# Linear attention on one core: an inverse ahead of the gelu phase, a value projection ahead of the MLP's later products

## What is computed

```python
for i in range(8):                                   # layers
    residual = x
    Q  = elu(x @ Wq[i] + bq[i]) + 1                  # 128 -> 1024
    Kf = elu(x @ Wk[i] + bk[i]) + 1
    V  = x @ Wv[i] + bv[i]
    KV, sumK = sum_tokens(Kf * V), sum_tokens(Kf)
    Z  = 1.0 / (Q * sumK + 1e-06)                    # the "inverse"
    att = Q * KV * Z
    y = gelu(att @ Wo[i] + bo[i])
    x = layer_norm(y + residual)
    h = gelu(x @ W1[i] + b1[i])                      # 128 -> 512
    x = layer_norm(gelu(h @ W2[i] + b2[i]) + x)
```

## Time and profile before

| | us |
|---|---|
| median of three runs | 4429.74 |
| profiled execution | 4422.76 |
| its span | 4421.0 |
| stage of linear attention (624 to 3066) | 2442 |

### The profile page before, as it was taken

How to read it: one execution, slowest core, us unless ns; L and a number is a source line. 1 busy time by engine, 2 the same in 40 slices (tenths; PEclk the granted TensorE clock), 3 DMA queues, 4 the chain that set the end, 5 groups by cost and what they waited for, 6 DMA issues and landing times.

```text
span 4421.0 us, 65537 instructions
## 1 busy us (share of the span) xinstructions
PE 3926.3 (89%) x15924; PEld 2196.2 (50%) x15924; DVE 3355.7 (76%) x10808; ACT 3129.1 (71%) x5783; POOL 1507.2 (34%) x2843
## 2 busy tenths in 40 slices
PE   5688879999999999999999999998698659999976
PEld 3466744444444444444444444443365447777745
DVE  5898579888878888788788887886666756665668
ACT  3455348999989899999899898998142426666654
POOL 2222124444444344444444344443210113333320
PEclk8888789999999999999999999999799779999988
DMA  2212110010000000000000000000000001111100
GB/s 54 34 30 40 19 24 1 1 22 3 10 16 1 17 9 1 21 6 1 23 3 8 18 1 16 11 1 1 0 1 1 0 14 44 45 44 41 43 6 19
DMA packets 152078, 71.90 MB, mean 16 GB/s; under 512 B 109576, under 2 KB 142684, under 8 KB 151666
## 3 DMA queue, kind: packets, MB, share of 16 engines
q1 hardware_dynamic: 144738, 63.96, 5.9%
q10 hardware_dynamic: 6928, 3.41, 0.3%
HBM read 54.55 MB, written 12.80 MB: 15 GB/s over the span
## 4 chain that ended last, share of the span: by engine, by line
PE 62%; DVE 15%; ACT 12%; issue 7%; POOL 1%; DMA 1%; ACTq 0%; DVEq 0%; SPq 0%; POOLq 0%
PE bank L2013 20%; PE bank L2028 7%; PE bank L2797 5%; PE bank L2057 5%; PE bank L2067 3%; PE bank L2830 2%; DVE arena L1460 2%; PE bank L613 2%; DVE arena L1464 2%; ACT L2151 2%; ACT arena L2105 2%; ACT arena L2108 2%; ACT arena L2117 2%; ACT arena L2104 2%; PE bank L2857 1%
## 5 line engine op out<-in xcount | busy, mean ns | idle before, releaser
L2013 PE MATMUL bank<-arena 128*128 128x512 f32 x3072 | 1422.5, 596 | 13.5 <-DVE arena L2194 12.0
L2013 PEld LDWEIGHTS bank<-arena 128*128 128x128 f32 x3072 | 585.9, 191 | 756.3 <-issue 722.3
L2254 POOL TENSOR_SCALAR arena<-arena 128x256 f32<-128x256 f32 x1024 | 480.4, 479 | 1190.9 <-DVE arena L2187 1190.9
L2028 PE MATMUL bank<-arena 128*128 128x512 f32 x1024 | 525.0, 604 | 62.7 <-DVE arena L2217 62.4
L2176 DVE SCALAR_TENSOR_TENSOR arena<-arena 128x256 f32<-128x256 f32 x1024 | 394.2, 422 | 195.8 <-ACT arena L2105 188.6
L2217 DVE SCALAR_TENSOR_TENSOR arena<-arena 128x256 f32<-128x256 f32 x1024 | 492.2, 525 | 13.7 <-issue 12.7
L2194 DVE SCALAR_TENSOR_TENSOR arena<-bank,bv,arena 128x256 f32<-128x256 f32 x1024 | 445.4, 473 | 0.0
L2104 ACT ACTIVATE arena<-bank,bqk 128x512 f32<-128x512 f32 x512 | 347.9, 680 | 76.9 <-PE bank L2013 68.4
L2187 DVE SCALAR_TENSOR_TENSOR arena<-bank,bq,arena 128x512 f32<-128x512 f32 x512 | 384.3, 751 | 18.1
L2117 ACT ACTIVATE arena<-arena,const_table 128x512 f32<-128x512 f32 x512 | 374.6, 732 | 0.0
L2108 ACT ACTIVATE arena<-bank,bqk 128x512 f32<-128x512 f32 x512 | 353.7, 691 | 0.9 <-PE bank L2013 0.8
(11 more groups left out here) (389 smaller groups left out, 7193.9 us busy)
## 6 DMA issues: line engine op xcount, KB each, us to landing
arena<-packed_dram SPq DMA_DIRECT2D x96, 96.0 KB
arena<-packed_dram SPq DMA_DIRECT2D x32, 288.0 KB
arena<-diag_dram SPq DMA_DIRECT2D x16, 256.0 KB, 3.8
arena<-in_L_attn_Wk_dram SPq DMA_DIRECT2D x16, 256.0 KB, 3.5
arena<-in_L_attn_Wq_dram SPq DMA_DIRECT2D x16, 256.0 KB, 4.2
arena<-in_L_attn_Wv_dram SPq DMA_DIRECT2D x16, 256.0 KB, 4.9
arena<-in_L_attn_Wo_dram SPq DMA_DIRECT2D x8, 512.0 KB, 3.9
arena<-in_L_attn_W_dram SPq DMA_DIRECT2D x16, 256.0 KB, 2.9
```

Of the source, the lines that this page charges most:

```text
L2013: nc.tensor.matmul(bank[:, RING1[m % 5], :], w1p[k][:, i * P:(i + 1) * P], zT_of(g), start=True, stop=True).then_inc(a1_proj.sem, 1)
L2028: nc.tensor.matmul(bank[:, 6, :], wo1[:, i, :], a1_att[:, i % 4, :], start=(i == 0), stop=(i == NB1 - 1)).then_inc(a1_outd.sem, 1)
L2254: last = nc.gpsimd.tensor_scalar(a, a, 1.0, a1_ksum[:, i % 4, b:b + 1], ALU.add, ALU.mult)
```

## The change

Two steps change their place in the lists of a turn; no operation is added or removed. On ScalarE `inv_act(2)` stands ahead of the gelu phase of the turn (behind exp 4) and no more behind exp 5. On TensorE the value product of block 5 stands directly behind its key and query products, ahead of hidden products 1 to 3, and no more behind them.

```diff
                 for w in range(NB1):
-                    pe.append((0, proj_pe(w, "kq" if w == 5 else "kqv")))
+                    pe.append((0, proj_pe(w)))
...
                     if w == 5:
-                        pe += [(2, h_pe((1, 2, 3))), (0, proj_pe(5, "v")), (3, turn_in_pe(1))]
+                        pe += [(2, h_pe((1, 2, 3))), (3, turn_in_pe(1))]
                         of(pe, out_pe, 0)
...
                     act.append((0, exp_act(w)))
                     if w == 4:
+                        of(act, inv_act, 2)
                         act += [(1, gelu_table_act), (3, h2_act), (1, y_act), (2, h_act), (1, exp_table_act)]
-                    if w == 5:
-                        of(act, inv_act, 2)
                     if w == 6:
                         of(act, inv_act, 3)
                         act.append((3, norm_act(1)))
```

## The result

| | before | after |
|---|---|---|
| median | 4427.72 us | 4468.36 us |
| span of the profiled execution | 4421.0 us | 4465.3 us |
| first to last gelu table load (63 turns) | 2391.34 us | 2430.09 us |

The change makes the kernel slower: ratio 1.009, 95% interval 1.0072 to 1.0107. The medians lie 40.6 us apart. Of the 44.3 us between the two spans 3.25 us lie ahead of the stage, where both kernels run the same code (ScalarE's first table load of the stage is at 623.79 us before and at 627.04 us after), and about 1 us lies behind the stage's last gelu table load.

A forecast was written before the change was run, and what follows sets the result against it. ScalarE's loop of 37.41 us bounds the turn, TensorE's 37.18 close behind; the change makes TensorE's 38.47. Terms 29.7 + 11.7 + 1.4 + 5 + 1 = 48.8 us on the 4429.74 median give 4479 us, range 4458 to 4508.

The forecast's parts named there:

- 28 turns without bias copies: Four turns per layer in layers 2 to 8: from 37.41 to 38.47 us, +1.06 each, 29.7 in all.
- 21 turns with them: Three turns per layer with ScalarE's bias copies: 113.74 to 115.41 us, +1.67 per layer, 11.7 in all.
- 7 layer ends: Turns over the layer loop's end: +0.2 us each, 1.4 in all, each bounded by 0 and 1.29.
- 6 turns of layer 1: Layer 1's turns of 37.02 us, partly shorter: +0.56 to +1.06 each where full, 5 us taken for the six.
- filling of the pipeline: The first new inverse adds about 1 us at the start of the pipeline.
- The ring: Loop exp 4, inverse, gelu phase, exp 5, VectorE, out product 2, projections, exp 4: 17.87 + 16.33 + 1.14 + 3.13 = 38.47 us.
- What out product 2 waits for: On TensorE: it waits for exp 5 through feature 5 and att 2, not for block 2's inverse, ended 0.87 us earlier.
- The value product: Block 5's, on TensorE ahead of hidden products 1 to 3: fills a wait, costs nothing, at most its 0.86 us.
- The clock: TensorE's granted clock: no falls expected behind about 1.5 us idle; the skill's rule would give 4585 us.
- Rival (a): TensorE's clock falls at the longer wait: one turn in three, 4514 us, chance 0.09; every turn, 4585 us, chance 0.01.
- signs: In the new profile: exp 0 waits 0.7 to 0.8 us, exp 4 about 0.2, hidden products 0.2 to 0.6.
- rival (b): No difference: ScalarE's loop of 37.41 us stays the bound, 4430 us; chance 0.07.

The follow-up runs named there:

- the fastest: Changed kernel plus att 2 ahead of feature 5, inverse 5 behind exp 0, inverse 2 ahead of exp 4: 4373.38 us; with later weight transfer 4363.03 us.

## Why the prediction was right, step by step

The forecast was 4479 us, the measured median 4468.36, inside the range; slower, as 0.87 of the chance said. Of the 10.6 us by which the forecast is too high, 2.0 are in the median that it stands on (4429.74, against 4427.72 with one run more), the rest in the sum. The terms, by the turns of the two profiled executions:

| term | forecast | measured |
|---|---|---|
| 28 turns without bias copies | +29.7 | +29.8 |
| 21 turns with them | +11.7 | +11.7 |
| 7 layer ends | +1.4 | -6.7 |
| 6 turns of layer 1 | +5 | +4.7 |
| filling of the pipeline | +1 | +1.3 |
| draining (last turn) | none | -0.7 |
| sum | +48.8 | +40.1 |

**The ring.** 38.47 us for a full turn was the sum of four distances, and each stands in the profile after as it was put: 17.87, 16.33, 1.14 and 3.13 (exp 4 at 2302.03 to the load at 2305.16). The bias copies vanished in ScalarE's new slack. All 49 full turns of layers 2 to 8 are 38.46 to 38.48.

**What out product 2 waits for.** Right, and shown from both sides: with exp 5 and feature 5 taken out of its way the loss is gone, at the same early inverse; and with the inverse's half alone the loss is all there.

**The value product.** The prediction said that it costs nothing since it fills a wait. That holds in the changed kernel (38.47 with it and without it), and its other bound, at most its 0.86, is seen on the kernel before, where it costs 0.5 to 0.6 us a turn on average (0.41 to 0.76).

**The clock.** The idle grew to 1.52 us (1.53 forecast) in every full turn, no full turn is longer than 38.48, and the trace's clock rows show no fall in them. Rival (a) is out. By the Trainium skill's section "HAM oscillation — how this bites in real kernels" ("TensorE: Matmul & The Clock Gate") a repeated wait can make each pass start cold; this loop's wait of 1.52 us didn't. In that section's example the wait of a pass is longer than the 2 us of matmuls in it, while here 1.52 us stand in a pass of 38.47, so the prediction stretched the rule to a case that the section doesn't describe.

**Small misses among the signs.** Exp 0 waited 0.53 us for TensorE, not 0.7 to 0.8: the norm's step before it had itself waited for TensorE's transposes, which moved ScalarE 0.2 nearer. Exp 4 waited 0.11 us, not 0.2. The hidden products waited 0.30 (from 2304.33 + 2.57 to 2307.20), inside the 0.2 to 0.6. The copies' 0.47 is 0.50 by the prediction's own 37.91 and 37.41, which its sum used, and the 0.45 us of slack in rival (b) stands in no row.

**The term that was mis-sized: the layer ends.** I had put them at +0.2 each: ScalarE gets to the jump 1.29 sooner and gives it back before the next load. Both halves of that hold (19.55 to 18.49, and 17.65 to 18.93 from exp 0 to the load). Missing was that the stop itself isn't a constant. Over the six ends with a jump, ScalarE's stops sum to 22.85 us before and 16.71 after, 6.14 less. From exp 0 to the next load two of the six ends before took 19.22 us instead of 17.65, 3.1 us together, with TensorE's clock falling behind idle stretches of 2.61 and 2.96 us there; after, one end was 0.88 and one 0.16 over its 18.93. These two, 6.1 us of shorter stops and 2.1 us less behind fallen clocks, are the 8 us by which this term was too high; the turns have no part in it. With the weights moved away from the jump, five of six layer ends before (41.20 to 41.56) are as long as those after (41.14 to 41.44), near the +0.2 that I had forecast, and the difference of the stops is 2.2 us instead of 6.1. So most of it needs the weight transfer at the jump. Why the transfer adds about 1.4 us to ScalarE's stop where it arrives 19.55 behind the load, about 0.7 at 18.49 and nothing that shows at 18.29 (with inverse 5 behind exp 0) stays open: the traffic runs at all three instants.

## What to carry to other kernels

Write the turn as rings: follow each wait back until the same step of the next turn, sum the distances, and do it for every engine, since the longest ring is the turn and the runner-up says how much slack an edit has. An operation moved ahead of a phase costs its length less the slack of the ring that the phase is in (1.29 - 0.23 = 1.06 us here), even if every engine on the path shows idle time; here it did no good without the consumer that can use it early. When several orders are good, try them in pairs: here an early inverse and an early att 2 each lose alone; beside the inverse of block 5 behind exp 0, which gains 1.0% alone, they take another 0.45 to 0.57 us off each full turn, though longer layer ends take about half of that back (1.1 to 1.2% gained in all). Moving a transfer off the loop's end brought 10 us on the kernel before (ratio 0.9975) and about as much on the fastest.

## What the runs showed of the hardware

ScalarE, where it jumps back at the end of the loop, stood 1.94 to 2.24 us with nothing to wait for (changed kernel, quiet DMA engines; 2.20 to 2.93 in the kernel before). With 768 KB of weights moved in beside it, it stood 2.54 to 3.22 and 3.46 to 4.11, but only 1.85 to 2.15 where it came at 18.29 us behind the load, amid the same transfer. TensorE at its own jump stood 1.68 to 2.30 us where it came at 18.03. Where it came 1.8 us sooner it stood 3.58 to 4.19 (three kernels with att 2 first), and 2.73 to 3.29 without the transfer; at 18.92, with the transfer, it stood 3.52 to 4.36 (att 2 first, late inverse).

The same stop can then bring TensorE's clock down: six matmuls behind a stop of 1.98 us took 4.53 us, those behind 4.12 us took 5.48, against 2.84 behind 1.96. The length of the stop doesn't decide it alone: in the fastest kernel the clock fell behind one of 2.73 us and not behind one of 3.29.
